# Moving the second score pair and the slot scores in the steady stage of an attention-plus-MLP kernel

## The chip, the cores and the metric

The kernel runs on one core of one Trainium2 chip, and the metric is the device time of one execution in microseconds. The core has five engines that run their own instruction lists and meet only at semaphores: TensorE (PE in the profile, PEld for its weight loads), VectorE (DVE), ScalarE (ACT), GpSimd (POOL) and SyncE (SP, which here only starts DMAs).

## The reference

Eight sequences of 256 tokens with 256 features go through a layer norm, and then two branches that are both added to the input:

```python
xn = _layernorm(x)
# attention branch, 16 heads of 128, 64 slots per head
q, k = rope(xn @ Wq.T), rope(xn @ Wk.T);  v = xn @ Wv.T;  g = xn @ Wg.T
s  = clip(xn @ Ws1.T @ Ws2.T + bs2, -32, 32)          # 64 slot scores a head
es, enz = exp(s), exp(-cumlogsumexp(s))
A  = where(mask, q @ k.T * DK ** -0.5, 0)
qv = softmax(enz * (A @ es))
W2 = where(mask, (qv * enz) @ es.T, 0)
o  = W2 @ v
attn = (o * rsqrt(mean(o * o) + EPS) * g_norm_weight * g * sigmoid(g)) @ Wo.T
# MLP branch, 2048 wide, 4-bit weights with a scale for each block of 32
mlp  = (gelu(xn @ Wg4.T) * (xn @ Wu4.T)) @ Wd4.T
out  = x + attn + mlp
```

All of it is float32. Where the kernel uses the faster fp32r operands it splits each factor into a high and a low part and adds three products.

## The kernel before

The work is cut into 32 stages. A stage is one pair of heads together with one eighth of the MLP (hp, 0 to 7), for one pair of sequences, that is 512 tokens (bp, 0 to 3); its number is st = 4·hp + bp. Stage 0 and stage 31 are written out by hand. Stages 1 to 30 run one function `stage(hp, bp)` on each engine, and the order of the calls in it is the order of the instructions on that engine. The five lists are independent of each other, and nothing schedules them. Each helper begins with the semaphore waits it needs and ends with an increment. So an instruction that waits holds up all that stands behind it on its engine.

These are the pieces that the change and the prediction speak of, with the names of the helpers:

- `scores(st, bp, i, hp)` (PE, lines 319 and 321) multiplies queries by keys for head i // 2 and sequence i % 2, in plain float32, so that each instruction is recorded as two passes. Scores 0 and 2 are written to the PSUM bank sc[0] (bank4), scores 1 and 3 to sc[1] (bank5). Scores 2 and 3, the second pair, need the banks back from scores 0 and 1.
- `score_diagonal(st, i)` (DVE, line 980) copies and masks the two diagonal blocks of score i out of its bank, and `off_diagonal(st, i)` (ACT, line 759) waits for it and copies the third block. Its increment of A_off gives the bank back.
- `mlp_up` (PE, lines 219 to 221, operand wgu) computes four tiles into banks 0 to 3: gate and up of unit 0 (tiles 0 and 1), gate and up of unit 1 (tiles 2 and 3). `gate_square` (ACT, line 782), `gate_arg` (DVE, line 1077), `gate_tanh` (ACT, line 787), `gate_gelu` (DVE, line 1082) and `hidden` (DVE, line 1088) are the gelu of a unit, each waiting for the one before.
- `gate_scale` and `gate_o` (DVE, lines 1002 and 1010) scale the attention output of the stage before, `gated_transpose` (PE, line 398) transposes it, and `gated_hi` (ACT, line 777) and `gated_lo` (DVE, line 1018) split the result. The split reads the banks rg[0] and rg[1].
- `slot_scores` (PE, line 304) computes the slot scores of the next stage into sc[0], once A_off shows that the copies of score 2 are done. `clip` (DVE, line 1025) and `slot_exp` (ACT, line 740) follow.
- `project_vg` (PE, operand wvg) computes four value/gate tiles of the next stage, here called v/g tiles. Tile 0 needs gate_gelu of unit 0, and tile 1 needs hidden of unit 0.
- `slot_reads` (PE, lines 332 and 335) writes rg[0], so it waits for gated_hi and gated_lo of head 0 (ogT_hi, ogT_lo) and for all four A_off.

The weights of the next head pair are prepared in between: in a stage with bp = 1, POOL's `dequantise` (line 1421) and ACT's `split_hi` of the output weights (line 703) stand ahead of off_diagonal 2. In a stage with bp = 3 ACT has `split_hi` of the v/g weights ahead of off_diagonal 2, and `split_hi` of the q/k weights between off_diagonal 2 and off_diagonal 3. Both orders are in ACT's `stage`.

Of the kernel before, what the change touches and what calls it, by code (L numbers as in the profile page):

```python
# [59 lines left out]
def build(nc, x, w_qkvg, w_packed, w_scaled, w_slot, w_slot1, g_norm, rope_tab, out):  # L60
    with ExitStack() as ctx:
# [203 lines left out]
        def _(pe):  # L265
# [46 lines left out]
            def scores(st, bp, i, hp):  # L312

                h, b = i // 2, i % 2
                if b == 0:
                    pe.wait_ge(roped, 4 * st + 2 * h + 2)
                dst = sc[b]
                t0 = b * T
                pe.matmul(dst[:, 0:T], qkT[:, 2 * h + 1, t0:t0 + P], qkT[:, 2 * h, t0:t0 + T],  # L319
                          start=True, stop=True)  # L320
                pe.matmul(dst[:, T:T + P], qkT[:, 2 * h + 1, t0 + P:t0 + T], qkT[:, 2 * h, t0 + P:t0 + T],  # L321
                          start=True, stop=True).then_inc(A_full, 1)
# [248 lines left out]
            def stage(hp, bp):  # L571
                st = 4 * hp + bp
                nbp = (bp + 1) % BP
                nhp = hp + 1 if bp == BP - 1 else hp
                php = hp - 1 if bp == 0 else hp


                prep = 3 if st == 1 else None
                for i in (0, 1):
                    pe.wait_ge(W_diag, 2 * st - 1 + i)  # L580
                    scores(st, bp, i, hp)
                if st == 1:
                    pe.wait_ge(cos_done, 4 * st + 4)
                    slot_inner(2, pj[3])
                mlp_up(st, bp, hp, 0)
                mlp_up(st, bp, hp, 1)
                for i in (2, 3):
                    pe.wait_ge(A_off, 4 * st + i - 1)
                    scores(st, bp, i, hp)
                mlp_up(st, bp, hp, 2)  # L590
                if st == 1:
                    pe.wait_ge(h1_done, 6)
                    pe.wait_ge(h1_lo, 3)
                mlp_up(st, bp, hp, 3)
                gated_transpose(st)
                pe.wait_ge(A_off, 4 * st + 3)
                slot_scores(st, nbp, nhp)
                project_vg(st + 1, nbp, nhp, 0, True)
                project_vg(st + 1, nbp, nhp, 1, True)
                pe.wait_ge(ogT_hi, 2 * st - 1)  # L600
                pe.wait_ge(ogT_lo, 2 * st - 1)
                slot_reads(st, rg[0])
                slot_states(st, bp)
                outputs(st, 0, php, None)
                project_vg(st + 1, nbp, nhp, 2, True)
                if prep:
                    pe.wait_ge(clip_done, st + 2)
                    transpose_x(prep, 0, sc[0])
                slot_rows(st)
                if prep:  # L610
                    x_split(KT * prep + 1)
                    transpose_x(prep, 1, sc[0])
                outputs(st, 1, php, st + 1)
                project_vg(st + 1, nbp, nhp, 3, True)
                pe.wait_ge(acc_done, 2 * st - 1)
                slot_softmax(st, rg[1])
                project_qk(st + 1, nbp, nhp, 0)
                if prep:
                    slot_inner(prep, sc[0])
                project_qk(st + 1, nbp, nhp, 1)  # L620
                project_qk(st + 1, nbp, nhp, 2)
                project_qk(st + 1, nbp, nhp, 3)
                pe.wait_ge(qe_ready, st + 1)
                pe.wait_ge(clip_done, st + 2)
                if prep:
                    pe.wait_ge(h1_done, 2 * prep + 2)
                    pe.wait_ge(h1_lo, prep + 1)
                slot_weights(st, bp, sc)
                carried(st)
                pe.wait_ge(cos_done, 4 * st + 5)  # L630
                pe.wait_ge(es_ready, st + 2)
                slot_transpose(pj[0], esT[nbp % 2])
                values(st, bp, 0)
                values(st, bp, 1)
# [3 lines left out]
            st, bp, hp = LAST, LAST_BP, HP - 1  # L638
# [44 lines left out]
        def _(act):  # L683
# [73 lines left out]
            def off_diagonal(st, i):  # L757
                act.wait_ge(A_diag, 4 * st + i + 1)
                act.activation(At[i][:, 1, :], sc[i % 2][:, P:2 * P], ACT.Copy, scale=SCALE).then_inc(A_off, 1)  # L759
# [114 lines left out]
            def stage(hp, bp):  # L874
                st = 4 * hp + bp
# [14 lines left out]
                    prepare_scales(hp + 1)  # L890
                if bp == 3 and more:
                    split_hi(hp + 1, W_VG)
                off_diagonal(st, 2)
                if bp == 3 and more:
                    split_hi(hp + 1, W_QK)
                off_diagonal(st, 3)
                gate_square(st, 1)
                gated_hi(st, 0)
                gated_hi(st, 1)
                gate_tanh(st, 1)  # L900
# [68 lines left out]
        def _(dve):  # L969
# [271 lines left out]
            def stage(hp, bp):  # L1241
# [11 lines left out]
                gate_arg(st, 0)  # L1253
                gate_scale(st)
                gate_o(npar, 0)
                score_diagonal(st, 2)
                gate_o(npar, 1)
                gate_gelu(st, 0)
                score_diagonal(st, 3)
                hidden(st, 0)  # L1260
                gate_arg(st, 1)
                if st == 1:
                    x_stats(prep)
                gated_lo(st, 0)
# [307 lines left out]
```

## Time and profile before

| | us |
|---|---|
| median of three runs | 1087.41 (1087.01 to 1087.88) |
| the profiled execution, its own time | 1087.74 |
| its span in the trace | 1086.0 |
| PE busy | 1072.1 (99% of the span), 7176 matmul passes |
| DVE busy | 920.1 (85%) |
| ACT busy | 653.7 (60%) |
| POOL busy | 420.3 (39%) |

TensorE's granted clock is full speed (9 in every one of the page's 40 slices, 0.998 in the mean). All times in the trace are counted from the start of the span. Three stages serve as samples below: stage 13 (bp = 1) begins at 462.50 us, stage 14 (bp = 2) at 495.30 us and stage 15 (bp = 3) at 528.10 us. In a row of the timeline the columns are the start, the time from the first start to the last end of what the row merges, the engine, the line, the operation, what is written and read, the shape, and how many were merged. In brackets stands the idle time before it and what ended it. One instruction may start a little before the one ahead of it on its engine has ended.

### The profile page before, as it was taken

Reading aid. Unit: us, or ns where it says so; the run is one execution under the profiler, and the core shown is the slowest. Engines: PE = TensorE matmul, PEld = TensorE weight load, DVE = VectorE, ACT = ScalarE, POOL = GpSimd, SP = SyncE. Lnnn points to the kernel's source line nnn. Section 1 sums busy time; section 2 is a strip of 40 time slices with the busy share of each in tenths; the row PEclk is TensorE's granted clock in tenths of the full one; section 3 lists DMA queues with packets and bytes.
Section 4 is the critical chain, followed back from the end, with each engine's and each line's share of the span. In section 5 each row is a group of like instructions: output and inputs, shape, how many; then the busy total and the mean of one; then the engine's idle time right before and its main releaser. Section 6 shows DMA issues by size and latency. Waiting matters only on the chain.

```text
span 1086.0 us, 20566 instructions
## 1 busy us (share of the span) xinstructions
PE 1072.1 (99%) x7176; PEld 923.7 (85%) x7176; DVE 920.1 (85%) x1680; ACT 653.7 (60%) x2111; POOL 420.3 (39%) x308
## 2 busy tenths in 40 slices
PE   8899999999999999999999999999999999999998
PEld 7688888888888888888888888888888888888887
DVE  6898988888888888889888898889888889888886
ACT  4666565666655666565756556656565666656653
POOL 5353252433523355232642316343253432524331
PEclk9999999999999999999999999999999999999999
DMA  5020000200002000020000200002000010000001
GB/s 171 1 78 4 1 2 1 75 6 1 1 1 81 1 2 1 2 80 2 1 1 2 80 2 2 1 1 80 1 1 1 15 67 1 1 2 1 20 21 40
DMA packets 9542, 23.06 MB, mean 21 GB/s; under 512 B 864, under 2 KB 5856, under 8 KB 8544
## 3 DMA queue, kind: packets, MB, share of 16 engines
q1 hardware_dynamic: 9440, 21.76, 5.8%
q8 instruction: 57, 0.93, 0.4%
q14 instruction: 45, 0.37, 0.1%
HBM read 19.66 MB, written 2.10 MB: 20 GB/s over the span
## 4 chain that ended last, share of the span: by engine, by line
PE 92%; DVE 2%; issue 1%; ACT 0%; POOL 0%; POOLq 0%; DVEq 0%
PE bank L219 21%; PE bank L221 21%; PE bank L220 21%; PE bank L389 5%; PE bank L319 5%; PE bank L360 3%; PE bank L332 3%; PE bank L398 3%; PE bank L321 2%; PE bank L309 2%; PE bank L382 1%; PE bank L335 1%; PE bank L369 1%; PE bank L344 1%; PE bank L351 1%
## 5 line engine op out<-in xcount | busy, mean ns | idle before, releaser
L1437 POOL TENSOR_TENSOR inter_lo<-ffb,inter_hi 128x512 fp32r<-128x512 f32 x62 | 79.5, 1306 | 447.5 <-ACT inter_hi L791 447.5
L1428 POOL TENSOR_TENSOR qkT<-ra,xs 128x512 f32<-128x512 f32 x128 | 165.6, 1295 | 132.2 <-DVE xs L1101 108.8
L754 ACT ACTIVATE sm<-bank,mx 128x64 f32<-128x64 f32 x256 | 76.5, 326 | 144.9 <-DVE mx L1057 144.9
L1101 DVE TENSOR_TENSOR xs<-xs,rope 128x512 f32<-128x512 f32 x128 | 130.4, 1019 | 0.0
L735 ACT ACTIVATE xs<-bank 64x512 f32<-64x512 f32 x128 | 76.3, 596 | 75.4 <-PE bank L221 46.6
L1098 DVE TENSOR_TENSOR ra<-bank,rope 128x512 f32<-128x512 f32 x128 | 87.9, 687 | 36.4 <-ACT xs L736 34.6
L1046 DVE RECIPROCAL enzT<-enzT 128x256 f32<-128x256 f32 x64 | 111.6, 1744 | 0.0
L219 PE MATMUL bank<-xh,wgu_hi 128*128 128x512 f32 x256 | 105.4, 412 | 0.0
L219 PE MATMUL bank<-xh,wqk_hi 128*128 128x512 f32 x256 | 102.8, 402 | 1.1 <-DVE ffa L1082 1.1
L219 PE MATMUL bank<-wvg_hi,xh 128*128 128x512 f32 x256 | 101.0, 394 | 1.0 <-ACT xh L795 1.0
L221 PE MATMUL bank<-xh,wgu_lo 128*128 128x512 f32 x256 | 101.0, 395 | 0.0
L220 PE MATMUL bank<-wvg_lo,xh 128*128 128x512 f32 x256 | 100.5, 393 | 0.0
L221 PE MATMUL bank<-wvg_hi,xl 128*128 128x512 f32 x256 | 100.3, 392 | 0.0
L220 PE MATMUL bank<-xl,wgu_hi 128*128 128x512 f32 x256 | 100.3, 392 | 0.0
L221 PE MATMUL bank<-xh,wqk_lo 128*128 128x512 f32 x256 | 99.9, 390 | 0.0
L220 PE MATMUL bank<-xl,wqk_hi 128*128 128x512 f32 x256 | 99.6, 389 | 0.0
L759 ACT ACTIVATE At<-bank 128x128 f32<-128x128 f32 x128 | 35.4, 278 | 80.8 <-DVE At L980 77.1
L319 PE MATMUL bank<-qkT 128*128 128x256 f32 x256 | 77.5, 385 | 2.8 <-POOL qkT L1428 2.8
L219 PE MATMUL bank<-wod_hi,ogT_hi 128*128 128x256 f32 x256 | 77.9, 304 | 0.1
L736 ACT ACTIVATE xs<-bank 64x512 f32<-64x512 f32 x128 | 75.6, 591 | 1.5
L220 PE MATMUL bank<-wod_lo,ogT_hi 128*128 128x256 f32 x256 | 72.0, 281 | 0.0
L221 PE MATMUL bank<-wod_hi,ogT_lo 128*128 128x256 f32 x256 | 71.7, 280 | 0.0
(165 smaller groups left out, 3064.1 us busy)
## 6 DMA issues: line engine op xcount, KB each, us to landing
raw<-in_w_qkvg SPq DMA_DIRECT2D x7, 1024.0 KB, 7.4
scaled<-in_w_scaled SPq DMA_DIRECT2D x8, 640.0 KB, 8.5
packed<-in_w_packed SPq DMA_DIRECT2D x8, 384.0 KB, 3.1
acc<-in_x SPq DMA_DIRECT2D x4, 512.0 KB, 8.4
out<-acc SPq DMA_DIRECT2D x3, 512.0 KB, 3.0
raw<-in_w_qkvg SPq DMA_DIRECT2D x2, 512.0 KB, 6.7
ws_raw<-in_w_slot SPq DMA_DIRECT2D x8, 48.0 KB, 2.9
rope<-in_rope_tab SPq DMA_DIRECT2D x1, 256.0 KB, 8.0
```

The lines of the kernel that those rows point to most:

```text
L219: pe.matmul(dst, stat[0], mov[0], start=start, stop=False)
L220: pe.matmul(dst, stat[0], mov[1], start=False, stop=False)
L221: return pe.matmul(dst, stat[1], mov[0], start=False, stop=stop)
L319: pe.matmul(dst[:, 0:T], qkT[:, 2 * h + 1, t0:t0 + P], qkT[:, 2 * h, t0:t0 + T], start=True, stop=True)
L735: act.activation(xs[i % 2][0:64, :], pj[i][64:128, :], ACT.Copy)
L736: act.activation(xs[i % 2][64:128, :], pj[i][0:64, :], ACT.Copy).then_inc(swapped, 1)
L754: ins = act.activation(sm[:, c], src[:, c], ACT.Exp, bias=mx[:, g:g + 1], accum_out=ssum[:, g:g + 1])
L1046: dve.reciprocal(enzT[par][:, c], enzT[par][:, c]).then_inc(enz_ready, 1)
L1098: dve.tensor_tensor(two(ra[i % 2][:, :]), two(pj[i][:, :]), cos, ALU.mult).then_inc(cos_done, 1)
L1101: dve.tensor_tensor(two(xs[i % 2][:, :]), two(xs[i % 2][:, :]), sin, ALU.mult).then_inc(sin_done, 1)
L1428: pool.tensor_tensor(qkT[:, i, :], ra[i % 2][:, :], xs[i % 2][:, :], ALU.add).then_inc(roped, 1)
L1437: pool.tensor_tensor(dst[1][e], ffb[e][:, :], dst[0][e].bitcast(F32), ALU.subtract).then_inc(inter_lo, 1)
```

## The change

Nothing is added or taken away; seven calls move within `stage`, on three engines. On PE, scores 2 and 3 move from between MLP tiles 1 and 2 to behind tile 3, directly ahead of the gated transposes, and the slot scores move from ahead of v/g tile 0 to between tiles 0 and 1. On ACT, the square of unit 1 moves ahead of off_diagonal 2 and 3. On DVE, score_diagonal 2 and 3 move behind gate_arg of unit 1.

```diff
 # PE
                 mlp_up(st, bp, hp, 0)
                 mlp_up(st, bp, hp, 1)
-                for i in (2, 3):
-                    pe.wait_ge(A_off, 4 * st + i - 1)
-                    scores(st, bp, i, hp)
                 mlp_up(st, bp, hp, 2)
 ...
                 mlp_up(st, bp, hp, 3)
+                for i in (2, 3):
+                    pe.wait_ge(A_off, 4 * st + i - 1)
+                    scores(st, bp, i, hp)
                 gated_transpose(st)
+                project_vg(st + 1, nbp, nhp, 0, True)
                 pe.wait_ge(A_off, 4 * st + 3)
                 slot_scores(st, nbp, nhp)
-                project_vg(st + 1, nbp, nhp, 0, True)
                 project_vg(st + 1, nbp, nhp, 1, True)
 # ACT
+                gate_square(st, 1)
                 off_diagonal(st, 2)
                 if bp == 3 and more:
                     split_hi(hp + 1, W_QK)
                 off_diagonal(st, 3)
-                gate_square(st, 1)
 # DVE
                 gate_o(npar, 0)
-                score_diagonal(st, 2)
                 gate_o(npar, 1)
                 gate_gelu(st, 0)
-                score_diagonal(st, 3)
                 hidden(st, 0)
                 gate_arg(st, 1)
+                score_diagonal(st, 2)
+                score_diagonal(st, 3)
```

On PE, around the gated transposes (operand og), the slot scores (operand ws) and v/g tiles (operand wvg), a plus marks what stands there now and a minus what stood there before:

```order
 L398 MATMUL bank<-ident,og 128x128 x8
+L219 MATMUL bank<-wvg_hi,xh 128x512
+L220 MATMUL bank<-wvg_lo,xh 128x512
+L221 MATMUL bank<-wvg_hi,xl 128x512
+L219 MATMUL bank<-wvg_hi,xh 128x512
+L220 MATMUL bank<-wvg_lo,xh 128x512
+L221 MATMUL bank<-wvg_hi,xl 128x512
 L304 MATMUL bank<-h,ws 128x512
-L219 MATMUL bank<-wvg_hi,xh 128x512
-L220 MATMUL bank<-wvg_lo,xh 128x512
```

The lines with a minus are the start of v/g tile 0 at its old place: six matmuls now run between the transposes and the slot scores. On DVE, from the scaling of the attention output (og) to the gelu of unit 1, the score diagonals being the rows that write At:

```order
-L1010 SCALAR_TENSOR_TENSOR og<-bank,scal,G 128x128 x4
-L980 TENSOR_TENSOR At<-bank,mask_a 128x2x128
-L1010 SCALAR_TENSOR_TENSOR og<-bank,scal,G 128x128 x4
-L1082 SCALAR_TENSOR_TENSOR ffa<-ffb,bank 128x512
-L980 TENSOR_TENSOR At<-bank,mask_a 128x2x128
-L1088 TENSOR_TENSOR ffb<-bank,ffa 128x512
-L1077 SCALAR_TENSOR_TENSOR ffb<-ffa,bank 128x512
+L1010 SCALAR_TENSOR_TENSOR og<-bank,scal,G 128x128 x8
+L1082 SCALAR_TENSOR_TENSOR ffa<-ffb,bank 128x512
+L1088 TENSOR_TENSOR ffb<-bank,ffa 128x512
+L1077 SCALAR_TENSOR_TENSOR ffb<-ffa,bank 128x512
+L980 TENSOR_TENSOR At<-bank,mask_a 128x2x128 x2
```

Score diagonal 2 now has four scalings, a gelu, a product and a gate_arg ahead of it that stood behind it. On ACT, in a stage with bp = 3, where the copies of the scores write At and the weight split writes wqk_hi:

```order
 L703 ACTIVATE wvg_hi<-raw 128x1024
+L782 ACTIVATE ffa<-bank 128x512
 L759 ACTIVATE At<-bank 128x128
 L703 ACTIVATE wqk_hi<-raw 128x1024
 L759 ACTIVATE At<-bank 128x128
-L782 ACTIVATE ffa<-bank 128x512
 L777 ACTIVATE ogT_hi<-bank 128x512 x2
```

The square of unit 1 goes first. The split of the q/k weights stays between the two copies of scores, and the split of the transposed output (ogT_hi) stays behind both.

## Rows read from the trace of the kernel before

**Rows 1.** Waits of PE over the whole span: total us, times, longest.
```profile
PE bank L319 <- POOL qkT L1428: 2.8, 2, 2.3
```

**Rows 2.** Timeline of PE in stage 13.
```profile
467.67 0.39 PE L321 MATMUL bank<-qkT 128*128 128x128 f32 x2
467.81 0.47 PE L219 MATMUL bank<-xh,wgu_hi 128*128 128x512 f32 x1
...
470.65 1.03 PE L398 MATMUL bank<-ident,og 128*128 128x128 f32 x8
471.44 0.48 PE L304 MATMUL bank<-h,ws 96*128 96x512 f32 x1
471.76 0.40 PE L219 MATMUL bank<-wvg_hi,xh 128*128 128x512 f32 x1
...
474.60 0.65 PE L332 MATMUL bank<-At,esJ 128*64 128x256 f32 x4
```

**Rows 3.** Timeline of PE in stage 14.
```profile
521.22 0.39 PE L221 MATMUL bank<-xh,wqk_lo 128*128 128x512 f32 x1
...
523.94 0.39 PE L221 MATMUL bank<-xh,wqk_lo 128*128 128x512 f32 x1
```

**Rows 4.** Timeline of DVE in stage 15.
```profile
533.37 0.17 DVE L1002 TENSOR_TENSOR scal<-rstd,rs 128x8 f32<-128x8 f32 x1 [0.84 <-POOL rstd L1433]
533.57 1.13 DVE L1010 SCALAR_TENSOR_TENSOR og<-bank,scal,G 128x128 f32<-128x128 f32 x4
534.61 0.42 DVE L980 TENSOR_TENSOR At<-bank,mask_a 128x256 f32<-128x256 f32 x1
534.94 1.12 DVE L1010 SCALAR_TENSOR_TENSOR og<-bank,scal,G 128x128 f32<-128x128 f32 x4
535.98 0.68 DVE L1082 SCALAR_TENSOR_TENSOR ffa<-ffb,bank 128x512 f32<-128x512 f32 x1
536.57 0.42 DVE L980 TENSOR_TENSOR At<-bank,mask_a 128x256 f32<-128x256 f32 x1
```

**Rows 5.** Timeline of DVE in stage 13.
```profile
467.74 0.69 DVE L1002 TENSOR_TENSOR scal<-rstd,rs 128x8 f32<-128x8 f32 x1 [1.01 <-POOL rstd L1433]
468.46 1.13 DVE L1010 SCALAR_TENSOR_TENSOR og<-bank,scal,G 128x128 f32<-128x128 f32 x4
```

**Rows 6.** Timeline of DVE in stage 14.
```profile
500.72 1.13 DVE L1010 SCALAR_TENSOR_TENSOR og<-bank,scal,G 128x128 f32<-128x128 f32 x4
```

**Rows 7.** Timeline of ACT in stage 15.
```profile
535.06 0.28 ACT L759 ACTIVATE At<-bank 128x128 f32<-128x128 f32 x1 [0.92 <-DVE At L980]
535.24 1.05 ACT L703 ACTIVATE wqk_hi<-raw 128x1024 fp32r<-128x1024 f32 x1
```

**Rows 8.** Groups of ACT instructions by line: busy us, mean ns, idle before.
```profile
L777 ACT ACTIVATE ogT_hi<-bank 128x512 fp32r<-128x512 f32 x62 | 33.9, 611 | 0.2 <-PE bank L398 0.2
```

**Rows 9.** Timeline of PE in stage 15.
```profile
540.19 0.65 PE L332 MATMUL bank<-At,esJ 128*64 128x256 f32 x4
```

**Rows 10.** Timeline, end of stage 0: ACT's last read, then PE.
```profile
48.53 0.24 ACT L754 ACTIVATION_READ_ACCUMULATOR sm<-bank,mx 128x1 f32 x1
...
48.84 0.43 PE L351 MATMUL bank<-ident,sm 128*128 128x128 f32 x2
```

**Rows 11.** Timeline in stage 1: DVE's split, then PE.
```profile
76.20 0.68 DVE L1018 TENSOR_TENSOR ogT_lo<-bank,ogT_hi 128x512 fp32r<-128x512 f32 x1
...
76.46 0.39 PE L221 MATMUL bank<-wvg_hi,xl 128*128 128x512 f32 x1
...
76.98 0.65 PE L332 MATMUL bank<-At,esJ 128*64 128x256 f32 x4
```

**Rows 12.** Waits of DVE over the whole span, for softmax_max.
```profile
DVE mx L1057 <- PE bank L344: 28.9, 30, 1.4
```

**Rows 13.** Timeline of POOL in stage 13.
```profile
467.67 1.43 POOL L1421 TENSOR_TENSOR raw<-packed,scaled 128x256 f32<-128x256 f16 x2
470.36 2.40 POOL L1407 TENSOR_TENSOR wod_lo<-raw,wod_hi 128x1024 fp32r<-128x1024 f32 x1 [1.25 <-ACT wod_hi L703]
```

## The prediction, before the run

> **What bounds the kernel now.** I first read the waits of PE over the whole span. The longest entry is 2.8 us in two waits [rows 1], the other entries are smaller, and none falls in the thirty looped stages as far as that view tells. So PE sets the time, and the time is the sum of the distances from one matmul's start to the next. Second, I read PE's timeline of a stage, not the durations but the distances. Twelve matmuls of 512 columns in the middle of a long run of their kind take 523.94 − 521.22 = 2.72 us [rows 3]. The twelve of MLP tiles 2 and 3, which follow the plain float32 scores, take 470.65 − 467.81 = 2.84 us [rows 2]. Third, I read DVE and ACT in the same stage for what PE is about to wait for. None of their own idle time costs anything now. What counts is how long before PE needs a result it is there.
>
> **What the change removes.** Work is moved only. PE switches from float32 scores to fp32r tiles once less per stage, since scores and transposes, both float32, now stand together. The 12 matmuls behind the lost switch should take 2.72 us and not 2.84, which gives 0.12. Against it, the first fp32r matmul starts 467.81 − 467.67 = 0.14 us after the first of the two last float32 passes. The passes lie 0.11 apart (0.39 for two that overlap, of some 0.28 each), so it starts 0.03 behind the second, where another float32 pass would start 0.11 behind it. That gives back 0.08. The gain is 0.04 us a stage, 1.2 us in 30 stages. The bounds are 0 (v/g tile 0 inherits the slow start) and 0.10 (half of the recovery of another switch too), so 0 to 3.0 us; I take 1.2, which is what the rows give directly.
>
> **What it adds: later diagonals.** PE has the scores 2 and 3 done well before DVE gets to them, so DVE's list decides. Stage 15 as the sample [rows 4]: gate_o of head 0 starts at 533.57 and takes until 534.61, where the second gate_o can now start. A gate_o takes 535.98 − 534.94 = 1.04, so gelu starts at 535.65. The product needs its result and starts after its end (0.68) and a handover of 0.04, at 536.37. A 512-wide operation lets the next start after 536.57 − 535.98 = 0.59 to 0.60, so gate_arg starts at 536.97 (its square is early now: ACT has it done once tile 2 and the first weight split are). Diagonal 2 runs from 537.56 to 537.98, diagonal 3 starts 534.94 − 534.61 = 0.33 later and ends at 538.31. Against gate_o's start that is 4.41 for the end of diagonal 2 and 4.74 for the end of diagonal 3, in every stage but the first.
>
> ACT takes off_diagonal 0.03 after the diagonal's end (534.61 + 0.42 = 535.03, start 535.06) and needs 0.28 [rows 4, 7]. From there two PE waits follow.
>
> *Wait 1, slot scores.* Before, they start 0.79 after the transposes [rows 2]. Now six v/g matmuls stand between: 0.32 for the first (471.76 − 471.44) and five of 0.23, 1.47 together. In stage 13 they are due at 471.44 − 0.04 + 1.47 = 472.87. gate_o starts there at 468.46 [rows 5], so diagonal 2 ends at 472.87 and the ACT copy at 472.87 + 0.03 + 0.28 = 473.18. From ACT's end to a PE matmul that waited for it passed 48.84 − 48.77 = 0.07 us [rows 10]. The slot scores start at 473.25: PE waits 0.38 us. In stage 14 gate_o starts at 500.72 [rows 6]; the copy is there at 505.44, PE could start at 505.51, and the old place is 471.44 − 462.50 = 8.94 behind the stage's start, 504.24, so it is due at 504.24 − 0.04 + 1.47 = 505.67 [rows 2]: no wait, with 0.16 to spare. Stage 15: the copy ends at 538.29, and PE is due at 540.19 − (474.60 − 471.44) + 1.43 = 538.46 [rows 2, 9]: just no wait. The difference is stage 13's gate_scale of 0.69 us in place of 0.17 [rows 4, 5]. Every stage with bp = 1 has it; without stage 1 these are 7. Cost 7 × 0.38 = 2.7 us. Queued behind the slot scores is all of PE's list, v/g tile 1 first, so nothing hides it. Bounds: 0.25 (each DVE handover 0.02 to 0.03 shorter) and 0.50, so 1.8 to 3.5 us.
>
> *Wait 2, slot reads.* They need gated_lo of head 0, which needs ACT's gated_hi behind off_diagonal 3. In stage 15 the q/k split stands between the two copies: off_diagonal 2 at 538.01, the split 0.18 later at 538.19, and the next instruction 0.10 before the end of its 1.05, at 539.14 (the overlap of 535.06 + 0.28 against 535.24) [rows 7]. Before, the split ran while ACT waited for diagonal 3, hidden. That cover is gone, since the diagonals are now 0.33 apart and not 1.96. gated_hi starts 0.18 later at 539.32 and takes 0.61 [rows 8]; gated_lo starts at 539.96 and ends 0.68 later at 540.64 [rows 11]. From DVE's end to slot reads, which carry several waits, passed 76.98 − 76.88 = 0.10 [rows 11]. They start at 540.74 and were due at 540.19 − 0.04 = 540.15 [rows 9]: PE waits 0.59 us. Seven stages have this split (3, 7, ... 27): 4.1 us. Bounds 0.40 and 0.75: 2.8 to 5.3 us. In stage 14, without the split, off_diagonal 3 ends at 505.46 + 0.31 = 505.77, gated_hi runs to 506.27 and gated_lo to 506.98, so slot reads could start at 507.08 and are due at 504.24 + 3.16 − 0.04 = 507.36: no wait. In stage 13 all is 0.54 later against the stage, but slot reads are late by the 0.38 of wait 1: gated_lo ends at 474.72, and PE is due at 474.56 + 0.38 = 474.94. No second wait.
>
> *Stage 1.* Slot reads already wait there for gated_lo: they start 0.52 after the last matmul, where the usual step is 474.60 − 471.44 less 0.32 and eleven of 0.23, so 0.31 [rows 2, 11]. gate_arg no longer waits for the square, so DVE comes 0.2 us sooner and so does PE: 0.2 us gained, between 0 and 0.3.
>
> **The sum.** Two waits 2.7 + 4.1 = 6.8, less 1.2, less 0.2: 5.4 us more. The profiled execution took 1087.74, 0.33 above the median of the runs, 1087.41; it becomes 1093.1, and the median 1092.8.
>
> DVE is behind by 0.7 us (stage 14) to 1.5 us (stage 15) at gated_lo. I cost that at nothing later: before softmax_max, about 7 us on, DVE waited for PE in 30 stages, 28.9 us in all, about 1 us in each [rows 12], and the delay goes into that and into the idle 0.2 to 0.3 us before smaller operations. If that cover were gone, PE would wait for the exponentials at the softmax transposes, by no more than a few tenths in the bp = 3 stages.
>
> **A rule against the trace.** DVE's gate_scale reads two SBUF tensors of eight columns and took 0.69 us beside POOL's dequantise, 0.17 without it [rows 4, 5, 13]; it ended 0.03 after the first of the two POOL instructions did. The Trainium skill, "SBUF — State Buffer", section "SBUF: two separate sides", says that DVE and GpSimd share one port pair under an exclusive lock, that a DVE operation with two SBUF inputs waits the whole GpSimd instruction out, and that others don't. By that rule DVE's diagonals, products and splits, which read one PSUM operand, stay as costed, but the two scans of stage 15 don't. A reading in which the lock held for all of DVE would give rival D.
>
> **Rivals.**
> A, no PE wait appears: not slower. The place is off_diagonal 2 in the bp = 1 stages and the q/k split in the bp = 3 stages; the point is that the copies come at least 0.38 and 0.59 us earlier than I place them. For it: stages 14 and 15 leave 0.16 and 0.07 at the slot scores. Against: DVE's chain is made of work it must do. It gives 1087.4 − 1.4 = 1086.0, and 1084.2 with the upper bound of the gain.
> B, one of the waits is real and the other is not: 1087.4 − 1.4 + 2.7 = 1088.7 or + 4.1 = 1090.1. For it: each rests on its own chain.
> C, the waits are there and the delay is not absorbed in the bp = 3 stages. POOL's low split of q/k waits for ACT's split, so it runs from about 539.31 to 541.71, and the dequantise pair behind it, twice as wide as the one in rows 13 and so by estimate 2.9 us, until 544.6. DVE comes to its two scans, which read two SBUF operands, after five 512-wide operations and a short one, at 539.96 + 5 × 0.6 + 0.4 = 543.4, so they would be 1.2 us late, as much as DVE's idle before softmax_max. With 0.3 of it reaching PE, 7 × 0.3 = 2.1 more; if the 0.16 at the slot scores of the 15 stages with bp = 0 and 2 is lost and 0.1 waited, 1.5 more: 1094.3 to 1096.4.
> D, the lock takes all of DVE: the split of 2.40 us would start 0.08 after ACT's, at 539.31, and hold gated_lo until 541.71, 1.75 us later: 7 × 1.75 = 12 more, 1105. Against it: in stage 13 the gelu, diagonal and products ran at their usual durations beside such a split (470.36 to 472.76) [rows 13].
>
> **How the numbers follow.** My forecast, both waits, 0.66: 1092.8, own range 1090.6 to 1095.2 from the bounds. A 0.10, B 0.11, C 0.11, D 0.02. 80% range: with A, D and the lower half of B outside, 1089.5 to 1095.6. A run of this kernel tells 0.2% (2.2 us) from no change, so faster means under 1085.2 and slower over 1089.6: faster is a third of A, 0.03; same is the rest of A and half of B, 0.12; slower 0.85.
>
> **What the profile would show.** In the waits of PE, line 304 waits for ACT's line 759 seven times, of some 0.4 us, and line 332 for DVE's line 1018 seven times, of some 0.6. Stages with bp = 0 and 2 are 0.04 us shorter than 528.10 − 495.30 = 32.80. Line 782 no longer holds gate_arg up. ACT's line 777 no longer starts right behind a square. I am wrong if the long stages are others, if diagonal 2 doesn't end 4.4 us after gate_o's start, or if the stages without a wait get longer.

## The result, and the profile after

| | before | after |
|---|---|---|
| median, us | 1087.51 (1087.01 to 1088.0) | 1095.02 (1094.14 to 1095.09) |
| the profiled execution, its own time | 1087.74 | 1095.02 |
| its span | 1086.0 | 1093.0 |

The ratio is 1.0067, with a 95% interval of 1.0055 to 1.0079: the change makes the kernel slower. Of the five executions of after one took 6093.12 us; it counts in the median, but not in the range and the ratio. So the difference of the two medians, 7.5 us, is a little too large: the median of the other four is 1094.69, 7.2 us above before, and the ratio gives 7.3 (6.0 to 8.6). The prediction had 5.4. The time of before in this table is the median of the runs made beside those of after.

The page of after, its span, its busy times and the shares of the chain that ended last:

```profile
span 1093.0 us, 20566 instructions
...
PE 1074.8 (98%) x7176; PEld 925.2 (85%) x7176; DVE 925.8 (85%) x1680; ACT 654.5 (60%) x2111; POOL 419.5 (38%) x308
...
PE 74%; DVE 11%; issue 6%; POOL 3%; ACT 1%; DVEq 0%; POOLq 0%; ACTq 0%
```

In before, PE's share of that chain was 92%. DVE's busy time grew by 5.7 us with the same 1680 instructions, so some of them take longer. The granted clock is still full in all 40 slices. The waits of PE in after (engine, what it writes, line, releaser, then the total in us, how often, the longest one):

```profile
PE bank L332 <- ACT ogT_hi L777: 3.2, 7, 0.5
PE bank L319 <- POOL qkT L1428: 2.8, 2, 2.3
...
PE bank L304 <- ACT At L759: 1.2, 7, 0.2
```

Against [rows 1] there are two new entries, seven times each, at the two lines where they were forecast. Where they fall is read from the first scores of four successive stages, 13 to 16, on PE's timeline of after:

```profile
464.98 0.60 PE L319 MATMUL bank<-qkT 128*128 128x256 f32 x2
...
498.23 0.60 PE L319 MATMUL bank<-qkT 128*128 128x256 f32 x2
...
531.04 0.60 PE L319 MATMUL bank<-qkT 128*128 128x256 f32 x2
...
564.38 0.60 PE L319 MATMUL bank<-qkT 128*128 128x256 f32 x2
```

Stage 13 (bp = 1) takes 33.25 us, stage 14 (bp = 2) 32.81, stage 15 (bp = 3) 33.34; all took 32.79 to 32.81 before. Read in the same way, these are the means of all kernels, those of the experiments below too. The last column is the time from the first scores of stage 1 to those of stage 31, less that of before (989.60 us):

| kernel | bp 0 | bp 1 (5, 9, ... 29) | bp 2 | bp 3 | stage 1 | stages 1 to 30 |
|---|---|---|---|---|---|---|
| before | 32.80 | 32.79 | 32.80 | 32.80 | 38.41 | 0 |
| after | 32.81 | 33.26 | 32.82 | 33.35 | 38.25 | +7.0 |
| e1, split before off_diagonal 2 | 32.82 | 33.26 | 32.82 | 32.81 | 38.25 | +3.5 |
| e2, slot scores behind v/g tile 1 | 32.82 | 33.04 | 32.97 | 33.35 | 38.48 | +7.1 |
| e3, diagonals behind gelu of unit 0 | 32.80 | 32.80 | 32.80 | 32.80 | 38.50 | +0.1 |
| e4, only the scores moved | 32.78 | 32.84 | 32.78 | 32.78 | 38.78 | +0.3 |
| e5, only the slot scores moved | 32.83 | 33.06 | 32.83 | 32.83 | 38.39 | +2.6 |
| e6, wait alone ahead of v/g tile 1 | 32.81 | 33.27 | 32.99 | 33.37 | 38.45 | +8.9 |
| e7, only PE's order | 33.70 | 33.70 | 33.70 | 33.70 | 40.13 | +27.9 |
| e8, POOL behind gate_scale | 32.84 | 32.83 | 32.83 | 33.36 | 37.91 | +4.1 |
| e9, e1 and e8 | 32.83 | 32.84 | 32.83 | 32.83 | 37.91 | +0.4 |
| e10, e4 and e8 | 32.78 | 32.78 | 32.78 | 32.78 | 38.81 | −0.1 |

In before, after, e3, e4, e7 and e10 the stages of one bp agree within 0.04 us. In the others some scatter more: the bp = 0 stages of e8, where nothing waits, take 32.79 to 32.85. The last column leaves out what comes ahead of the loop. That part varies by itself: the first scores of stage 0 start at 31.3 to 31.6 us in six of the twelve profiled executions and at 30.6 to 30.8 in the other six.

After less before is 7 × 0.46 + 7 × 0.55 + 15 × 0.01 − 0.16 = 7.1 us from the rounded means, and 7.04 from the trace. The spans differ by 7.0 too.

**The wait at the slot scores, stage 13.** DVE's timeline of after, which answers to [rows 5] (times are 2.5 us later, since the stage begins at 464.98 and not 462.50):

```profile
470.20 0.69 DVE L1002 TENSOR_TENSOR scal<-rstd,rs 128x8 f32<-128x8 f32 x1 [1.01 <-POOL rstd L1433]
470.93 2.16 DVE L1010 SCALAR_TENSOR_TENSOR og<-bank,scal,G 128x128 f32<-128x128 f32 x8
473.01 0.67 DVE L1082 SCALAR_TENSOR_TENSOR ffa<-ffb,bank 128x512 f32<-128x512 f32 x1
473.71 0.69 DVE L1088 TENSOR_TENSOR ffb<-bank,ffa 128x512 f32<-128x512 f32 x1
474.32 0.68 DVE L1077 SCALAR_TENSOR_TENSOR ffb<-ffa,bank 128x512 f32<-128x512 f32 x1
474.92 0.75 DVE L980 TENSOR_TENSOR At<-bank,mask_a 128x256 f32<-128x256 f32 x2
```

The two diagonals are one row now. The first ends at 474.92 + 0.42 = 475.34, 4.41 behind gate_o's start at 470.93, as worked out. ACT's copies in after:

```profile
472.64 0.58 ACT L782 ACTIVATE ffa<-bank 128x512 f32<-128x512 f32 x1
...
475.37 0.61 ACT L759 ACTIVATE At<-bank 128x128 f32<-128x128 f32 x2 [2.14 <-DVE At L980]
```

ACT had idled for 2.14 us, so it is DVE's list that comes late. The first copy ends at 475.37 + 0.28 = 475.65, and PE in after:

```profile
475.12 0.40 PE L221 MATMUL bank<-wvg_hi,xl 128*128 128x512 f32 x1
475.70 0.50 PE L304 MATMUL bank<-h,ws 96*128 96x512 f32 x1 [0.18 <-ACT At L759]
476.04 0.40 PE L219 MATMUL bank<-wvg_hi,xh 128*128 128x512 f32 x1
476.27 0.40 PE L220 MATMUL bank<-wvg_lo,xh 128*128 128x512 f32 x1
```

The bracket says 0.18. But an undisturbed step is 0.23, and this one is 0.58 (0.34 more by the unrounded starts): the slot scores start that much late. The matmul behind them then comes after 0.34 and not after 0.23. The wait costs 0.34 + 0.11 = 0.45 in all, more than its own length. PE's weight loads show where the 0.11 comes from. PEld in after, stage 13, the loads for the slot scores and for the matmul behind them:

```profile
475.70 0.19 PEld L304 LDWEIGHTS bank<-h,ws 96*128 96x128 f32 x1 [0.61 <-ACT At L759]
475.81 0.19 PEld L219 LDWEIGHTS bank<-wvg_hi,xh 128*128 128x128 f32 x1
```

In stage 14, without a wait, the load for the slot scores starts at 508.42, 0.19 ahead of its matmul. Here it waits with its matmul and starts with it, and the next load comes 0.11 behind it, 0.23 ahead of the matmul at 476.04.

In all seven stages gate_scale takes 0.69 or 0.70 us. In stage 13 it ends at 470.89, with the first of POOL's two dequantise instructions (470.87).

**The wait at the slot reads, stage 15.** ACT in after, the answer to [rows 7]:

```profile
540.96 0.28 ACT L759 ACTIVATE At<-bank 128x128 f32<-128x128 f32 x1 [3.39 <-DVE At L980]
541.13 1.05 ACT L703 ACTIVATE wqk_hi<-raw 128x1024 fp32r<-128x1024 f32 x1
542.08 0.27 ACT L759 ACTIVATE At<-bank 128x128 f32<-128x128 f32 x1
542.24 1.09 ACT L777 ACTIVATE ogT_hi<-bank 128x512 fp32r<-128x512 f32 x2
```

The split stands in the chain, as forecast. DVE and then PE in after, up to the slot reads:

```profile
542.87 0.69 DVE L1018 TENSOR_TENSOR ogT_lo<-bank,ogT_hi 128x512 fp32r<-128x512 f32 x1 [1.61 <-ACT ogT_hi L777]
```

```profile
542.81 0.39 PE L221 MATMUL bank<-wvg_hi,xl 128*128 128x512 f32 x1
543.66 0.65 PE L332 MATMUL bank<-At,esJ 128*64 128x256 f32 x4 [0.47 <-ACT ogT_hi L777]
```

gated_lo ends at 543.56, and the slot reads start 0.10 later. Without a wait they start 0.32 behind the last v/g matmul (474.28 to 474.60 in before), at 543.13: 0.53 late. The view puts the wait down to ACT's gated_hi, which had been ready since 542.84. What releases the slot reads is gated_lo, which itself sat 1.61 us waiting for that copy.

**The scans beside POOL.** POOL in after, stage 15, and the two scans of DVE, which took 1.27 us in before (second fence, from DVE's timeline of before) and take 2.16 now (third):

```profile
542.26 2.39 POOL L1407 TENSOR_TENSOR wqk_lo<-raw,wqk_hi 128x1024 fp32r<-128x1024 f32 x1 [2.73 <-ACT wqk_hi L703]
544.81 2.53 POOL L1417 TENSOR_TENSOR raw<-packed,scaled 128x512 f32<-128x512 f16 x2 [0.17 <-POOL wqk_lo L1407]
```

```profile
541.87 1.27 DVE L1040 TENSOR_TENSOR_SCAN enzT<-esT 128x256 f32<-128x256 f32 x2
```

```profile
546.32 2.16 DVE L1040 TENSOR_TENSOR_SCAN enzT<-esT 128x256 f32<-128x256 f32 x2
...
550.97 0.62 DVE L1057 TENSOR_REDUCE mx<-bank 128x8 f32<-128x512 f32 x1
```

The dequantise runs until 547.34 and the first scan overlaps it. The DVE waits before softmax_max show who paid: the last of these rows was 28.9 us in 30 waits before [rows 12].

```profile
DVE ra L1098 <- ACT xs L736: 30.2, 31, 1.9
...
DVE mx L1057 <- PE bank L344: 9.2, 16, 0.7
```

DVE's delay used up most of its idle time there (none is left in stage 15), and PE didn't wait at the softmax transposes.

### The profile page after: what moved, and what is told of

Read it like the earlier page. It is cut to its first block, busy times and chain, and to the rows that moved or that the text cites. A ratio compares the mean times of both kernels' runs of the same rounds, so it can differ in the third digit from the quotient of the medians.

```text
span 1093.0 us, 20566 instructions
## 1 busy us (share of the span) xinstructions
PE 1074.8 (98%) x7176; PEld 925.2 (85%) x7176; DVE 925.8 (85%) x1680; ACT 654.5 (60%) x2111; POOL 419.5 (38%) x308
## 4 chain that ended last, share of the span: by engine, by line
PE 74%; DVE 11%; issue 6%; POOL 3%; ACT 1%; DVEq 0%; POOLq 0%; ACTq 0%
PE bank L219 18%; PE bank L221 17%; PE bank L220 17%; PE bank L360 3%; PE bank L332 3%; PE bank L389 3%; PE bank L319 3%; DVE og L1010 3%; POOL rstd L1433 2%; DVE ra L1098 2%; PE bank L398 1%; PE bank L321 1%; PE bank L335 1%; PE bank L369 1%; DVE xs L1101 1%
## 5 line engine op out<-in xcount | busy, mean ns | idle before, releaser
L219 PE MATMUL bank<-wvg_hi,xh 128*128 128x512 f32 x256 | 103.6, 405 | 1.0 <-ACT xh L795 1.0
L219 PE MATMUL bank<-xh,wgu_hi 128*128 128x512 f32 x256 | 103.2, 403 | 0.0
```

The source lines that it names most:

```text
L219: pe.matmul(dst, stat[0], mov[0], start=start, stop=False)
```

## The experiments

Ten kernels ran. Each was compared with runs of before on its own chip: the medians were 1087.4 for e1 to e4, 1087.3 for e5 to e7, and 1087.62 for e8 to e10. The diffs are against after unless said otherwise, in the function `stage` of the engine named. The theory is that of the prediction: two waits in fourteen stages, one made by DVE's longer list together with gate_scale's 0.69 us, the other by the q/k split.

**e1_split_first** takes the split out of the chain (ACT):

```diff
                 gate_square(st, 1)
-                off_diagonal(st, 2)
                 if bp == 3 and more:
                     split_hi(hp + 1, W_QK)
+                off_diagonal(st, 2)
                 off_diagonal(st, 3)
```

> The changed kernel with one call moved on ACT: the split of the q/k weights stands ahead of off_diagonal 2 and not between off_diagonal 2 and 3. Theory (each of the two waits of PE has its own cause; the one at the slot reads of stages 3, 7 to 27 comes from the split between the two copies): gated_lo ends some 0.8 us earlier there, line 332 waits no more, the seven stages go from 33.35 to 32.8 us, and the kernel gets 7 x 0.55 = 3.9 us faster than the changed one: 1091.1. The seven stages with bp = 1 stay at 33.26. Rival (DVE is simply late in these stages, whatever ACT does): no change, 1095.0.

Measured 1090.6 us (1090.36 to 1092.02), ratio 1.0031 [1.0021, 1.0042]. The bp = 3 stages fall from 33.35 to 32.81 and the bp = 1 stages stay at 33.26. ACT in e1, stage 15, has the split done long before the diagonal:

```profile
535.26 1.05 ACT L703 ACTIVATE wqk_hi<-raw 128x1024 fp32r<-128x1024 f32 x1
538.76 0.61 ACT L759 ACTIVATE At<-bank 128x128 f32<-128x128 f32 x2 [2.45 <-DVE At L980]
539.26 1.09 ACT L777 ACTIVATE ogT_hi<-bank 128x512 fp32r<-128x512 f32 x2
```

In the waits of PE the entry of line 332 is gone and that of line 304 is unchanged. So the place of the split makes the second wait, and the two waits are independent. It is worth 7 × 0.53 = 3.7 us. The theory stands; its rival of 1095.0 is out.

**e8_pool_after_scale** takes the 0.5 us out of gate_scale (POOL):

```diff
                 if bp == 1:
+                    pool.wait_ge(scal_done, st)
                     dequantise(hp, W_OD)
```

> The changed kernel with one wait added on POOL, ahead of the dequantise in the stages with bp = 1: it waits for DVE's gate_scale, which now runs beside no POOL operation. Theory (the wait at the slot scores has its cause there: gate_scale takes 0.69 and not 0.17 us beside the dequantise, since both read two SBUF tensors): all of DVE's chain comes 0.52 us earlier in these stages, off_diagonal 2 is there 0.2 before it is due, line 304 waits no more, the stages go from 33.26 to 32.81: 7 x 0.45 = 3.2 us faster than the changed kernel, 1091.5. Rival (ACT's split of the output weights, which now comes up to 0.4 us later, holds the square of unit 1 and the copies behind it, so the stages stay long): 1094 to 1095.

Measured 1091.4 us (1091.26 to 1091.89), ratio 1.0036 [1.0022, 1.005]. The bp = 1 stages fall from 33.26 to 32.83, the bp = 3 stages stay. DVE and POOL in e8, stage 13:

```profile
468.29 0.17 DVE L1002 TENSOR_TENSOR scal<-rstd,rs 128x8 f32<-128x8 f32 x1 [1.00 <-POOL rstd L1433]
```

```profile
468.54 1.43 POOL L1421 TENSOR_TENSOR raw<-packed,scaled 128x256 f32<-128x256 f16 x2 [0.28 <-DVE scal L1002]
```

The same operation on 128 × 8 elements takes 0.17 us as soon as POOL's dequantise runs behind it and not beside it. So the 0.5 us come from POOL, and without them there is no first wait: its seven stages are then as short as the others (32.83 against 32.84 and 32.83).

**e9_both_causes** has both edits.

> The changed kernel with both causes taken away at their source, neither PE nor DVE touched: POOL's dequantise waits for gate_scale, and ACT's split of the q/k weights stands ahead of off_diagonal 2. Theory: 7.1 us faster than the changed kernel, all stages at 32.80 to 32.82, equal to the kernel before within 0.5: 1087.0 to 1088.0. Rival (a part of the loss has another cause): 1088.5 or more.

Measured 1087.27 us (1087.02 to 1088.05), ratio 0.9998 [0.9989, 1.0006], and both waits are gone from the waits of PE. Of the 7.0 us in stages 1 to 30, 6.6 are gone: the two causes are the loss, as far as these times can tell. Nothing is left of a gain. The steady stages take 32.83 or 32.84, which is 0.03 more than before and 0.02 more than the stages of after that don't wait. That is 0.9 us in 29 stages. Stage 1, 0.5 shorter than before, hides half of it. It is also more than e3 has with the same order on PE, and its cause stays open.

**e3_diag_behind_gelu** takes the list instead of its neighbours: the diagonals come 1.3 us earlier (DVE; the first ends 3.09 us behind gate_o's start in stage 13, not 4.41).

```diff
                 gate_gelu(st, 0)
-                hidden(st, 0)
-                gate_arg(st, 1)
                 score_diagonal(st, 2)
                 score_diagonal(st, 3)
+                hidden(st, 0)
+                gate_arg(st, 1)
```

> The changed kernel with the two score diagonals on DVE placed between the gelu of unit 0 and its product, two 512-wide operations earlier; PE and ACT as in the changed kernel. Theory: off_diagonal 2 ends 1.3 us earlier, the split of the q/k weights begins 1.3 us earlier, and both waits are gone: 7 us faster than the changed kernel and equal to the kernel before within 0.5, 1087.3 to 1088.1. Rival (the order on PE costs something itself): 1089 or more. Rival (the order on PE is worth the 0.04 us a stage of the prediction once nothing waits): 1086.2.

Measured 1087.82 us (1087.13 to 1088.04), ratio 1.0002 [0.9993, 1.0011]. Both waits are gone with PE's order that of after. So the order on PE needs no wait and need not cost anything; the place of the diagonals on DVE does. But it brings nothing either: the stages take 32.80, not 32.76.

**e4_scores_only** asks where the gain of the removed switch is. The scores are moved, the slot scores stand at their old place, and DVE takes the diagonals early:

```diff
 # PE
                 gated_transpose(st)
-                project_vg(st + 1, nbp, nhp, 0, True)
                 pe.wait_ge(A_off, 4 * st + 3)
                 slot_scores(st, nbp, nhp)
+                project_vg(st + 1, nbp, nhp, 0, True)
 # DVE
                 gate_o(npar, 1)
+                score_diagonal(st, 2)
                 gate_gelu(st, 0)
+                score_diagonal(st, 3)
                 hidden(st, 0)
                 gate_arg(st, 1)
-                score_diagonal(st, 2)
-                score_diagonal(st, 3)
```

> The second score pair moved as in the changed kernel, the slot scores left at their old place ahead of v/g tile 0; on DVE diagonal 2 stands ahead of the gelu of unit 0 and diagonal 3 behind it, on ACT the order of the changed kernel. Theory (the switch saved is worth 0.04 to 0.05 us a stage, the slot scores' move gives it back): 30 x 0.046 = 1.4 us faster than the kernel before, 1086.1, with no wait in a looped stage. Rival (PE's step after a switch shifts elsewhere, and the sum doesn't change): 1087.5.

Measured 1087.87 us (1087.14 to 1088.59), ratio 1.0003 [0.9994, 1.0012]: the 1086.1 wasn't there. Of the 0.04 us a stage, 0.02 is left where bp isn't 1, 0.4 us in all. The bp = 1 stages take 0.04 more each and stage 1 takes 0.38 more, so stages 1 to 30 come out 0.3 longer. **e5_slot_only** is the other half: before, with the slot scores alone moved (diff against before):

```diff
                 gated_transpose(st)
+                project_vg(st + 1, nbp, nhp, 0, True)
                 pe.wait_ge(A_off, 4 * st + 3)
                 slot_scores(st, nbp, nhp)
-                project_vg(st + 1, nbp, nhp, 0, True)
```

> The kernel before with the slot scores alone moved, from ahead of v/g tile 0 to between tiles 0 and 1; the rest as before, so off_diagonal 2 is long done when they are due. Theory (six matmuls take up the slow start behind the transposes, and the slot scores break the run of v/g tiles): 0.02 us a stage slower, 0.7 us in all, 1088.2, no wait. Rival (a single 96-row matmul costs the same anywhere): 1087.5.

Measured 1089.81 us (1089.36 to 1091.89), ratio 1.0025 [1.0015, 1.0034], more than the 1088.2 expected. The distances on PE from the start of a block to the start of the next show where the time goes in both. This is stage 14, in which PE waits for nothing. The column of before has the distances in ns, the others the differences to it:

| block | before | after | e4 | e5 |
|---|---|---|---|---|
| MLP tile 2 | 1473 | −113 | −113 | 0 |
| MLP tile 3 | 1375 | −9 | −8 | 0 |
| the last scores | 1229 | +81 | +81 | 0 |
| v/g tile 0 | 1385 | +86 | −6 | +87 |
| slot scores | 315 | −83 | +4 | −82 |
| v/g tile 1 | 1451 | +22 | 0 | +21 |
| q/k tiles 0 and 1, two tiles | 2830 | +24 | +24 | −1 |

The first three lines are the switch: −41 ns, the 0.04 of the prediction. The slot scores' place takes +25 in after: v/g tile 0 stands directly behind the transposes and takes over the slow start that the slot matmul had (+86 and −83), and v/g tile 1 takes 22 more. The first two numbers are much the same in e3 and e9. The third is not: it is 6 in e3 and 40 in e9, whose order on PE is that of after. So the place of the slot scores costs 12 to 47 ns, and what decides it wasn't found. The q/k tiles, 13 us later in the stage, take 24 ns more in after, e3 and e4, 7 more in e9, and nothing more in e5 and in e7. PE has the same order in after, e3, e7 and e9, and nothing waits at these tiles. So it isn't the order alone, and the cause stays open.

The 0.03 us a stage fit the expected 0.7 us. The larger part of e5's loss, 7 × 0.27 = 1.9 us, is in its bp = 1 stages, 33.06, where no wait was expected. PE in e5, stage 13:

```profile
471.37 1.03 PE L398 MATMUL bank<-ident,og 128*128 128x128 f32 x8
472.38 0.47 PE L219 MATMUL bank<-wvg_hi,xh 128*128 128x512 f32 x1
```

DVE's gelu of unit 0 in e5, which v/g tile 0 needs:

```profile
471.56 0.68 DVE L1082 SCALAR_TENSOR_TENSOR ffa<-ffb,bank 128x512 f32<-128x512 f32 x1
```

It ends at 472.24 and the tile starts 0.14 later; it was due at 472.16. The slot scores had covered that gelu. These are again the stages in which gate_scale takes 0.5 us longer. In after the gelu ends at 473.68 and the tile starts at 473.89, when it is due, so this wait doesn't show: the late scores come ahead of the tile, and no diagonal stands between the two gate_o.

**e2_slot_behind_vg1** puts the slot scores and their wait behind v/g tile 1 (PE):

```diff
+                project_vg(st + 1, nbp, nhp, 1, True)
                 pe.wait_ge(A_off, 4 * st + 3)
                 slot_scores(st, nbp, nhp)
-                project_vg(st + 1, nbp, nhp, 1, True)
```

> The changed kernel with one call moved on PE: the slot scores stand behind v/g tile 1 and not ahead of it, so that they are due 1.4 us later. DVE and ACT are as in the changed kernel. Theory: line 304 waits no more in stages 5, 9 to 29, these go from 33.26 to 32.8, 7 x 0.45 = 3.2 us faster than the changed kernel: 1091.8; the wait of the slot reads stays as it is. Rival (the wait moves on to what PE does next, since DVE is late for slot reads too): under 1 us faster, 1094 to 1095.

Measured 1094.5 us (1094.28 to 1094.95), ratio 1.0065 [1.0053, 1.0078]. This expectation of 1091.8 fell, and its rival (1094 to 1095) came true. PE in e2, stage 13:

```profile
477.22 0.39 PE L304 MATMUL bank<-h,ws 96*128 96x512 f32 x1
477.78 0.65 PE L332 MATMUL bank<-At,esJ 128*64 128x256 f32 x4 [0.17 <-issue]
```

The slot scores don't wait, but the slot reads right behind them start 0.56 later and not 0.32. They need gated_lo of head 0, DVE in e2:

```profile
476.98 0.69 DVE L1018 TENSOR_TENSOR ogT_lo<-bank,ogT_hi 128x512 fp32r<-128x512 f32 x1 [0.83 <-ACT ogT_hi L777]
```

It ends at 477.67. So the bp = 1 stages fall only to 33.04. And the bp = 2 stages grow from 32.82 to 32.99 (without stage 2, which stays at 32.82). There DVE's clip, in e2, now waits for the slot scores:

```profile
510.69 0.69 DVE L1025 TENSOR_SCALAR esT<-bank 128x512 f32<-128x512 f32 x1 [0.49 <-PE bank L304]
```

In after it started at 509.83 with no wait. softmax_max starts 19.80 us into the stage, not 19.21, and the softmax transposes, which need what follows from it, start 0.17 late. This is the place where the prediction saw DVE's delay reach PE if its cover went. In the bp = 2 stages of after about 0.59 − 0.17 = 0.4 us of that cover are left. What the bp = 1 stages win is lost here, and stages 1 to 30 take as long as in after.

**e6_wait_on_vg1** keeps the wait ahead of v/g tile 1 and moves the slot scores alone behind it (PE). It asks whether the extra 0.11 us belongs to the slot scores:

```diff
                 pe.wait_ge(A_off, 4 * st + 3)
-                slot_scores(st, nbp, nhp)
                 project_vg(st + 1, nbp, nhp, 1, True)
+                slot_scores(st, nbp, nhp)
```

> The changed kernel with the slot scores behind v/g tile 1, but PE's wait for off_diagonal 2 kept where it is, so that the first matmul of v/g tile 1 carries it. It asks what a wait costs beyond its own length: in the changed kernel's stage 13 the slot scores start 0.34 us late, and the matmul behind them starts 0.34 after and not 0.23. Theory (any fp32r matmul that had to wait has its own weights and the next ones not loaded ahead, so one step of 0.33 follows every wait): in stages 5, 9 to 29 the first matmul of tile 1 starts 0.34 late and the second 0.33 behind it, and the time is that of the changed kernel, 1095.0. Rival (the extra 0.1 belongs to the slot scores, a lone matmul with other weights): the second follows after 0.23, and the kernel is 0.7 us faster, 1094.3.

Measured 1096.09 us (two runs), ratio 1.0079 [1.006, 1.0097]. PE in e6, stage 13:

```profile
475.26 0.40 PE L221 MATMUL bank<-wvg_hi,xl 128*128 128x512 f32 x1
475.83 0.50 PE L219 MATMUL bank<-wvg_hi,xh 128*128 128x512 f32 x1 [0.17 <-ACT At L759]
476.17 0.40 PE L220 MATMUL bank<-wvg_lo,xh 128*128 128x512 f32 x1
```

An ordinary v/g matmul that waits is followed after 0.34 too. The theory had the weights not loaded ahead, and the load for line 219 waits with the matmul here as that for line 304 does in after. So the 0.11 belongs to the wait and not to the instruction. The time of 1095.0 that was expected was missed all the same. Stages 1 to 30 take 1.8 us more than in after, and 1.35 of it is in the bp = 2 stages at 32.99. They are like those of e2: the slot scores come later, and the clip waits 0.51 for them.

**e7_pe_only** has PE's order of after with the ACT and DVE of before (diff against after, DVE; on ACT the square stands behind off_diagonal 3 again):

```diff
                 gate_o(npar, 0)
+                score_diagonal(st, 2)
                 gate_o(npar, 1)
                 gate_gelu(st, 0)
+                score_diagonal(st, 3)
                 hidden(st, 0)
                 gate_arg(st, 1)
-                score_diagonal(st, 2)
-                score_diagonal(st, 3)
```

> PE's order as in the changed kernel, DVE and ACT as in the kernel before. Theory (DVE's order must follow PE's): diagonal 2 waits on DVE for scores that are done 2.7 us later and holds the second gate_o, so the transposes of head 1 come 0.6 us late and v/g tile 0 another 0.2: 0.8 us in each of 30 stages, 25 us slower than before, 1112. Rival (DVE's idle time of some 5 us a stage takes it up): under 1092.

Measured 1115.74 us (two runs), ratio 1.0259 [1.0241, 1.0278]. The first entry in its waits of PE:

```profile
PE bank L398 <- DVE og L1010: 13.8, 30, 0.5
```

Every stage takes 33.70, 0.9 more than before where 0.8 was expected, and stage 1 takes 1.7 more. DVE in e7, stage 13, stands at diagonal 2 until PE has computed the late scores, and the transposes then wait for the second gate_o:

```profile
481.79 0.42 DVE L980 TENSOR_TENSOR At<-bank,mask_a 128x256 f32<-128x256 f32 x1 [0.56 <-PE bank L321]
482.13 1.12 DVE L1010 SCALAR_TENSOR_TENSOR og<-bank,scal,G 128x128 f32<-128x128 f32 x4
```

So once PE's scores are late, the diagonals must leave their old place between the two gate_o; what the change got wrong is how far they went.

**e10_scores_only_pool** is e4 with the wait of e8, a try at a version that keeps e4's 0.02 us a stage.

> The kernel with only the score pair moved (slot scores at the old place, diagonal 2 ahead of and diagonal 3 behind the gelu) and POOL's dequantise waiting for gate_scale. There the stages with bp = 1 were 32.84 and the others 32.78, against 32.80 before. Theory (v/g tile 0 and the slot scores were held a little in the bp = 1 stages by results 0.16 to 0.20 us ahead of them): all stages at 32.78, 30 x 0.02 = 0.6 us faster than before at best: 1086.9, not to be told from it. Rival (nothing left): 1087.5 to 1087.9.

Measured 1087.38 us (1086.88 to 1087.77), ratio 0.9997 [0.9989, 1.0006]. All steady stages take 32.78. Those with bp = 1, 32.84 in e4, fell with the others, so that part of e4 came from POOL as well. But stage 1 takes 0.40 more than before, and stages 1 to 30 together only 0.1 less. That is no difference that these runs can tell. No kernel here beats before.

## Why the forecast was right in sign and 2 us short

| term | forecast, us | measured, us |
|---|---|---|
| wait at the slot scores | 7 × 0.38 = 2.7 | 7 × 0.44 = 3.1 |
| wait at the slot reads | 7 × 0.59 = 4.1 | 7 × 0.54 = 3.8 |
| the new order of PE (a switch less) | −1.2 | +0.3 |
| stage 1 | −0.2 | −0.2 |
| sum | 5.4 | 7.0 |

The measured terms are differences of stages in the one profiled execution. The waits count against the 32.81 of an undisturbed stage of after, and the order of PE is the 0.01 by which that stage is longer than before, in 29 stages. The rest of the 7.5 between the medians is none of these terms: by the ratio the difference is 7.3, and 7.0 lies in its interval.

The measured 1095.02 lies inside the forecast's own range, 1090.6 to 1095.2, but at its upper end. The range is narrower than the sum of the bounds that it is said to come from: those give 1.8 + 2.8 − 3.0 − 0.3 to 3.5 + 5.3, so 1088.7 to 1096.2, and the prediction doesn't say how it narrowed them. The two waits together came to 6.9, against 6.8. That they agree so well is partly luck, since one was too small by 0.4 and the other too large by 0.3. So nearly all of what is missing is the gain.

- **What bounds the kernel** held: only PE's steps and its waits moved the time, and DVE's 5.7 us of longer work cost PE nothing.
- **The wait at the slot scores** was right in place, cause and the seven stages, and too small in price. The start came 0.34 late (0.38 forecast, of which 0.04 was the gain that should have made PE early). The prediction silently took a wait to cost its own length, and that step failed. It costs 0.11 more: the weight load of a waiting matmul waits too, and the matmul behind it comes after 0.34 and not 0.23; e6 shows it on another matmul, and e8 takes both away.
- **The wait at the slot reads** was right within 0.05; e1 shows the split as its cause. The restart is no extra here: the slot reads and the block behind them (line 369) take 1.32 + 0.57 us with the wait and 1.35 + 0.54 without it. The forecast named line 1018 as the releaser in the view, and the view names ACT's line 777.
- **The gain of 0.04 a stage** is the step that failed most. The prediction took the 12 matmuls behind the lost switch and the 0.08 at the start, and that part is right (−41 ns). It gave the new place of the slot scores no price: +25 ns in after. Its own lower bound, 0 with "v/g tile 0 inherits the slow start", was the better value. The +24 ns at the q/k tiles was in no row read. The sum is no gain: the stages without a wait got 0.00 (bp 0) to 0.01 (bp 2) longer. That stages without a wait get longer is one of the signs by which the prediction said it would be wrong, and for this term it was.
- **The slack at the slot scores** was 0.16 in stage 14 by the forecast. In after the copy ends at 508.37, 0.07 more is the handover, and the slot scores start at 508.61: 0.17. For stage 15 the prediction has 0.07, but its own numbers give 538.46 − 538.29 − 0.07 = 0.10; in after it is 0.11. So neither stage waits there, as said.
- **Stage 1** gained its 0.2 in the way that was forecast: gate_arg no longer waits 0.23 for the square, gated_lo starts at 76.01 and not at 76.20, and the slot reads at 76.80 and not at 76.98. Over all stages line 782 holds gate_arg up 7 times for 1.6 us in all, against 37 times and 8.7 us before.
- **The exclusive port.** gate_scale's 0.69 us falls to 0.17 once POOL runs behind it (e8), and the two scans of stage 15 grow from 1.27 to 2.16 beside the dequantise, while the DVE operations with one PSUM operand beside POOL's split kept their durations (0.68 and 0.69 at 542.87 to 544.08, within POOL's 542.26 to 544.65). Over all of after, the 8 gate_scale beside a POOL instruction take 0.69 to 0.70 us and the 23 others 0.16 to 0.17. By the rule of the Trainium skill, "SBUF — State Buffer", section "SBUF: two separate sides", it is the DVE operations with two SBUF inputs, beside a GpSimd instruction that reads SBUF, that are locked out (those in a 2-port performance mode are named there too, and no run here tells anything of them). The trace agrees on both sides.
- **The rivals.** A (no wait) and B (one of them) fell: both waits stood in seven stages each. C came half true. Its scans are held up as it said (by 0.9 us, where it had 1.2), and DVE's idle before softmax_max shrank from 28.9 us to 9.2, but nothing of that reached PE. e2 shows that 0.6 us more would have. Its time, 1094.3 to 1096.4, holds the measured one, but for a reason that the traces don't show, so that is luck. D is out: DVE worked at its usual pace beside the split.

## What to carry to other kernels

Where an engine is busy to the last per cent, moving its producer's steps has no price until they pass a slack, and then costs the lateness in full and, at the 512-column matmuls here, a restart of 0.1 us beside it. So work out for each moved consumer the slack of its operands in every kind of stage, not in a typical one: here two of four kinds had none, each for a neighbour's instruction (a dequantise of POOL, a weight split on ACT) that the change didn't touch. And a switch between operand types that is removed at one place can reappear at the next, so sum the distances through the whole stage before a gain is booked.

## What the runs showed of the hardware

- Where PE doesn't wait, the step from one block to the next mostly repeats within a few ns from stage to stage (in before within 5 ns, but for MLP tiles 0 and 1, which take 2836 to 2855). It isn't always so: in e9 nothing waits in any steady stage, and v/g tile 1 takes 1455 to 1497 ns. So a difference of some 20 ns in one block between two kernels need not come from their order.
- A 512-column fp32r matmul that waited is followed by the next after 0.34 us, not 0.23 (after and e6). Its weight load waits too, and the next load starts only 0.11 behind it. At the slot reads, which are smaller, a wait adds nothing of the kind.
- Tiles 2 and 3 of the MLP behind fp32r tiles take 1.36 + 1.37 = 2.73 us (after), and 1.47 + 1.38 = 2.85 behind plain float32 scores (before).
- An 8-column DVE operation with two SBUF inputs takes 0.69 us beside POOL's dequantise and 0.17 without it (after and e8).
